# Window scores of a transformer block as 64x64 matmuls, four side by side, with one copy of kT and one signal per tile

## The reference, cut to what matters

```python
h = shift_token(x)
q, k, v = jnp.split(h @ wqkv, 3, axis=-1)          # 8 heads of 64
q, k = rotary_xpos(l2norm(q) * qs, l2norm(k) * ksc)
# windows of 64 tokens; keys are those of the window and of the one before
sim = jnp.einsum('bhwid,bhwjd->bhwij', bq, bk)
mask = (i < j) | (i > j + WINDOW) | (j == -1)
attn = jax.nn.softmax(jnp.where(mask, -jnp.finfo(sim.dtype).max, sim), axis=-1)
out = jnp.einsum('bhwij,bhwjd->bhwid', attn, bv)
x = x + o @ wo
```

## Time and profile before

| | |
|---|---|
| median of 3 runs | 2111.05 us (2105.78 to 2113.18) |
| profiled execution, span | 2108.0 us |
| instructions in it | 46234 |
| TensorE matmul, weight load | 1782.1 us (85%), 1504.1 us (71%) |
| VectorE, ScalarE, GpSimd | 1462.3, 1256.6, 1091.2 us |
| granted TensorE clock | 9 tenths or more in nearly all slices, 7 to 8 between the stacks |

### The profile page before, as it was taken

The page is one execution under the profiler, slowest core; times in us unless marked ns, Lnnn a source line. Parts: engine busy times, 40 slices in busy tenths (PEclk is TensorE's granted clock), DMA queues, the critical chain, the costliest instruction groups (busy, mean ns, idle before and its releaser), DMA issues.

```text
span 2108.0 us, 46234 instructions
## 1 busy us (share of the span) xinstructions
PE 1782.1 (85%) x14712; PEld 1504.1 (71%) x14712; DVE 1462.3 (69%) x3770; ACT 1256.6 (60%) x3443; POOL 1091.2 (52%) x1090
## 2 busy tenths in 40 slices
PE   1899999888999999747756759999998999999984
PEld 1787878777878788625534548878787788888873
DVE  6786868676868687455666548777776767677763
ACT  1686868675868686512311337676766667676771
POOL 3774747464747475321131247565655556665550
PEclk9999999999999999978978879999998999999997
DMA  7221212122112111031010031111112121212113
GB/s 249 85 68 40 48 38 54 44 73 60 45 38 48 41 45 35 12 123 40 0 40 20 10 78 45 39 48 43 46 50 74 39 65 37 49 34 50 33 35 103
DMA packets 183658, 111.91 MB, mean 53 GB/s; under 512 B 86720, under 2 KB 164128, under 8 KB 182944
## 3 DMA queue, kind: packets, MB, share of 16 engines
q1 hardware_dynamic: 183456, 109.12, 19.6%
HBM read 43.41 MB, written 23.42 MB: 32 GB/s over the span
## 4 chain that ended last, share of the span: by engine, by line
PE 69%; DVE 9%; issue 8%; ACT 7%; DMA 3%; SPq 3%; POOL 2%; DVEq 0%; POOLq 0%; ACTq 0%
PE QK L345 12%; PE OB L689 9%; PE SC L611 6%; PE TT L578 6%; PE SC L615 5%; PE VB L345 4%; PE QK L578 4%; PE OB L644 4%; PE TT L345 3%; PE SC L601 3%; ACT probs L1099 2%; PE OB L746 2%; PE VB L746 2%; PE OB L578 2%; PE VB L578 2%
## 5 line engine op out<-in xcount | busy, mean ns | idle before, releaser
L1099 ACT ACTIVATE probs<-SC,shift,qgain 128x128 f32<-128x128 f32 x1024 | 454.3, 457 | 105.1 <-DVE shift L898 104.9
L1225 POOL TENSOR_TENSOR ve<-mv,epsilon 128x1 f32<-128x1 f32 x128 | 24.3, 190 | 614.0 <-DVE mv L942 614.0
L345 PE MATMUL QK<-w_qkv,hT 128*128 128x512 f32 x768 | 227.4, 435 | 49.4 <-issue 16.5
L890 DVE TENSOR_REDUCE top<-SC 128x4 f32<-128x512 f32 x256 | 174.9, 683 | 99.8 <-PE SC L618 97.8
L1093 ACT ACTIVATE kT<-QK 64x512 f32<-64x512 f32 x256 | 150.9, 590 | 121.5 <-PE QK L578 120.0
L951 DVE TENSOR_TENSOR rope_c<-QK,rope 128x512 f32<-128x512 f32 x256 | 174.7, 682 | 68.8 <-PE QK L345 66.3
L578 PE MATMUL TT<-ident,probs 128*128 128x128 f32 x1280 | 193.3, 279 | 29.8 <-ACT probs L1099 23.1
L1238 POOL TENSOR_TENSOR rnorm<-clip,mhalf 128x8 f32<-128x8 f32 x128 | 211.5, 1653 | 12.7 <-DVE clip L907 12.4
L345 PEld LDWEIGHTS QK<-w_qkv,hT 128*128 128x128 f32 x768 | 146.3, 204 | 95.2 <-issue 42.3
L1247 POOL TENSOR_TENSOR qgain<-clip,mhalf 128x8 f32<-128x8 f32 x128 | 209.4, 1636 | 0.7 <-ACT probs L1099 0.5
L1099 ACT ACTIVATION_READ_ACCUMULATOR probs<-SC,shift,qgain 128x1 f32 x1024 | 208.1, 203 | 0.0
(11 more groups left out here) (141 smaller groups left out, 4361.1 us busy)
## 6 DMA issues: line engine op xcount, KB each, us to landing
v_prev<-v_own SPq DMA_DIRECT2D x256, 128.0 KB, 2.3
x_att<-stream SPq DMA_DIRECT2D x128, 64.0 KB, 2.1
h<-stream SPq DMA_DIRECT2D x256, 32.0 KB, 1.9
stream<-x_new SPq DMA_DIRECT2D x32, 256.0 KB
w_qkv<-qkv_d SPq DMA_DIRECT2D x3, 1536.0 KB, 6.5
h<-x_mid SPq DMA_DIRECT2D x128, 32.0 KB
h<-x_mid SPq DMA_DIRECT2D x128, 31.8 KB
rope<-rope_d SPq DMA_DIRECT2D x24, 128.0 KB, 3.3
```

What stands on the lines that cost most here:

```text
L345: last = mm(dst, fr(left(a)), fr(right(b)), start=(k == 0), stop=(k == 2))
L890: v.tensor_reduce(top[:, t.i % 2, 4 * half:4 * half + 4], SC[:, half * 512:half * 512 + 512].rearrange("q (h k) -> q h k", h=4), AX, ALU.m ...
L1099: last = nc.scalar.activation(probs[:, b, hd, :], SC[:, hd * P:hd * P + P], ACT.Exp, bias=shift[:, b, hd:hd + 1], scale=qgain[:, b, hd:hd ...
```

## The change

The scores of a tile are computed in one place, ahead of the products with v, as 16 matmuls of 64 channels x 64 queries x 128 keys (64 keys for the first window of a sequence). For chunk c, window w and head e of the pair, the weights are partitions 64e to 64e + 63 of qT and the output goes to partitions 64w to 64w + 63 of SC, bank e. The even heads' scores so stand in the first bank and the odd heads' in the second, and every later step that goes by heads is reordered: probs and psums are in the order 0, 2, 4, 6, 1, 3, 5, 7, and qgain, pT and rsums are picked to match. kT has no zeros; its four slots of 64 keys are the windows of two tiles, written by one copy of 128 partitions, and the previous window is reached by a slot step of -1 or 3. s_s goes up once per tile instead of twice.

```diff
-        kT = sb("kT", [P, 2, PAIRS, 2, P])
+        kT = sb("kT", [P, PAIRS, 4, WIN])
...
-            def scored(t, half):
+            def scored(t):
 
                 i, b = t.i, t.i % 2
-                sc = SC[:, :].rearrange("q (c e b k) -> q c e b k", c=PAIRS, e=2, b=2)
-                chunks = (2 * half, 2 * half + 1)
-                for c in chunks:
-                    last = mm(sc[:, c, :, 0, :], qT[:, b, c, :], kT[:, b, c, :, 0:64],
-                              start=False, stop=True, skip_group_check=True)
-                for c in chunks:
-                    if i:
-                        last = mm(sc[0:64, c, :, 1, :], qT[:, b, c, 0:64], kT[:, 1 - b, c, :, 64:128],
-                                  start=False, stop=True, skip_group_check=True)
-                for c in chunks:
-                    last = mm(sc[64:128, c, :, 1, :], qT[:, b, c, 64:128], kT[:, b, c, :, 64:128],
-                              start=False, stop=True, skip_group_check=True)
+                sc = SC[:, :].rearrange("q (e c s k) -> q e c s k", e=2, c=PAIRS, s=2)
+                for c in range(PAIRS):
+                    for w in range(2):
+                        for e in range(2):
+                            d, q = slice(64 * e, 64 * e + 64), slice(64 * w, 64 * w + 64)
+                            if w:
+                                keys = kT[d, c, 2 * b:2 * b + 2, :]
+                            elif not i:
+                                keys = kT[d, c, 2 * b:2 * b + 1, :]
+                            else:
+                                keys = kT[d, c, 2:0:-1, :] if b else kT[d, c, 0:4:3, :]
+                            last = mm(sc[q, e, c, 0:keys.shape[1], :], qT[d, b, c, q], keys,
+                                      start=False, stop=True, skip_group_check=True)
                 last.then_inc(s_s, 1)
...
                         need(pe, s_p, t.count(back=1, unit=2))
+                        pe.wait_ge(s_qT, t.count())
+                        pe.wait_ge(s_kT, t.count())
                         masked(t, 0)
                         masked(t, 1)
-                        pe.wait_ge(s_qT, t.count())
-                        pe.wait_ge(s_kT, t.count())
-                        scored(t, 0)
+                        scored(t)
...
-                                          pT[:, hd, 64 * w:64 * w + 64], v[:, t.i, hd * DH:hd * DH + DH],
+                                          pT[:, hd % 2 * 4 + hd // 2, 64 * w:64 * w + 64], v[:, t.i, hd * DH:hd * DH + DH],
...
-                    if t := tile(TQK):
-                        scored(t, 1)
...
-            v.memset(kT[:], 0.0).then_inc(s_zero, 1)
...
-                dve.wait_ge(s_s, t.count(unit=2) + (half - 1))
+                dve.wait_ge(s_s, t.count())
...
-                                       in1=qgain[:, t.i % 2, hd], op0=ALU.mult, op1=ALU.mult).then_inc(s_sh, 1)
+                                       in1=qgain[:, t.i % 2, :].rearrange("p (c e) -> p e c", e=2)[:, half], op0=ALU.mult, op1=ALU.mult).then_inc(s_sh, 1)
...
-                    v.tensor_tensor(o_n[:].rearrange("q (h d) -> q h d", h=HEADS),
-                                    OB[:, :].rearrange("q (h d) -> q h d", h=HEADS),
-                                    rsums[:, b, :].unsqueeze(2).to_broadcast([P, HEADS, DH]), ALU.mult).then_inc(s_on, 1)
+                    v.tensor_tensor(o_n[:].rearrange("q (c e d) -> q c e d", c=PAIRS, e=2),
+                                    OB[:, :].rearrange("q (c e d) -> q c e d", c=PAIRS, e=2),
+                                    rsums[:, b, :].rearrange("q (e c) -> q c e", e=2).unsqueeze(3).to_broadcast([P, PAIRS, 2, DH]),
+                                    ALU.mult).then_inc(s_on, 1)
...
-                    need(act, s_s, t.count(back=1, unit=2))
-                    for e in range(2):
-                        last = copy(kT[64 * e:64 * e + 64, b, :, e, :],
-                                    QK[64 * e:64 * e + 64, 512:1024].rearrange("d (c t) -> d c t", c=PAIRS))
-                    last.then_inc(s_kT, 1)
+                    need(act, s_s, t.count(back=1))
+                    copy(kT[:, :, 2 * b:2 * b + 2, :].rearrange("d c s k -> d c (s k)"),
+                         QK[:, 512:1024].rearrange("d (c t) -> d c t", c=PAIRS)).then_inc(s_kT, 1)
```

More of the change, by code:

```diff
@@ L1099, in exponentials @@
                     last = nc.scalar.activation(probs[:, b, hd, :], SC[:, hd * P:hd * P + P], ACT.Exp,
-                                                bias=shift[:, b, hd:hd + 1], scale=qgain[:, b, hd:hd + 1],
+                                                bias=shift[:, b, hd:hd + 1], scale=qgain[:, b, hd % 4 * 2 + half:hd % 4 * 2 + half + 1],
                                                 accum_out=psums[:, b, hd:hd + 1])
@@ L1275, in _ @@
             pipeline(pool, step, 1)
-ZEROED = 6
+ZEROED = 5
 N_CONST = 16 * 16
```

## The result

The changed kernel takes 2023.26 us (median of 4 runs, 2021.15 to 2025.16) against 2111.43 us (median of four runs of the kernel before, the three above and one more); the ratio is 0.9586, with a 95% interval of 0.9569 to 0.9602. The profiled execution's span is 2022.0 us, 86.0 less than the 2108.0 of the earlier trace rows.

What follows compares the result with a forecast made beforehand. It took a plain step of 10.39 us, a ring through TensorE and ScalarE's copies, as the bound. Per eight steps 5 x 0.67 + 0.3 + 1.0 + 0.45 = 5.1 us, times 16: 82 us, forecast 2028 us, range 1990 to 2080.

Steps and rivals of the forecast that it cites:

- Four abreast: Score matmuls on TensorE: 64x64 matmuls run four at a time, 0.86 us plus 0.33 for shape changes, 1.19 us.
- Rival A: Score matmuls run only two at a time, 0.86 us more per tile; 2135 us in all, chance 0.07.
- rival B: Score weight loads not hidden: rounds of 0.15 instead of 0.107 us, 0.35 us per tile; 2072 us, chance 0.15.
- Rival C: Score matmuls run one at a time, 3.42 + 0.33 us per tile; slower, 2357 us, chance 0.08.
- The point from which it loses: Time for all scores of a tile above which the changed kernel is slower than before: 1.8 us.
- o_n loses its cover: VectorE's o_n, no longer hidden behind the second half of the scores, ends 0.85 us after the products with v.
- TensorE's ring: TensorE's own work in a plain main-loop step, from one QKV product to the next: 9.67 us.
- VectorE's ring with GpSimd: Plain step: shift waits for GpSimd's q_r, and norm and hT wait behind shift, a loop of 9.65 us.
- Rival D: shift slips in before GpSimd's q_r and shape changes cost 0.1 us: plain step 9.45, whole 1997 us, chance 0.10.
- One copy of kT: ScalarE's kT copying falls from 1.18 to 0.60 us, so the copies no longer hold up the QKV product.
- The burst step: Step with a feed-forward burst: earlier transpose of o_n and no second kT copy, 1.0 us gained together.
- The step with the jump: Step at the loop's end: 0.45 us gained before the jump, while the 3.25 us wait for code stays.

Runs made afterwards that it cites:

- the halves: Changed kernel with the 64x64 scores split again, even heads before the products with v and odd heads behind: 2059.3 us, ratio 0.9761.
- runs of four: Changed kernel with the score matmuls reordered, four in a row in the same quarter of the array: 2230.9 us, ratio 1.0569.
- the two copies: Changed kernel with kT copied again as two pieces of 64 partitions: 2087.35 us, ratio 0.9888.
- runs of two: Changed kernel with the score matmuls reordered, two in a row in the same quarter of the array: 2026.48 us, ratio 0.9594.

## Why the prediction was right, point by point

- **Four abreast, and 1.19 us for all scores.** Right: 1.13 us. Rival A, two at a time, is excluded by the slots of the changed kernel and by the halves; rival B, rounds of 0.15 us, by the 0.109 us from one four to the next. Part 3 of the Trainium skill's page "TensorE: Matmul & The Clock Gate" would have weights load beside running matmuls only with another row group. The trace does not bear that out: the second four weight loads start at 518.15 to 518.17, between the first four matmul records (518.10 to 518.12) and the second (518.26 to 518.28), in quarters that share rows. Rival C, that 64-row matmuls exclude each other, is wrong as a rule, but a loss like it lies one loop order away: runs of four take 2.49 us, and that kernel is 120 us slower than the one before the change. The point from which it loses was put at 1.8 us for all scores; the two orders with 1.13 and 2.6 us lie on either side.
- **o_n loses its cover.** Right: expected to end 0.85 us after the products, found at 521.82 - 520.96 = 0.86, and TensorE waits 0.47.
- **TensorE's ring 9.67 us.** It is 9.54. The stretch from the start of o_n's transposes to the QKV product takes 2.62 and not 2.70 us, the one from the end of the products to those transposes 0.91 and not 0.95; none of the sum's terms is off by more than 0.1.
- **VectorE's ring with GpSimd 9.65 us.** It is 9.66. Rival D, in which this ring isn't there, is excluded: shift lasts 0.46 and 0.58 us above and ends with q_r. I took 9.72 for a plain step as if the two rings always disturbed each other; in fact they alternate. The mean gain of a plain step, first tiles among them, was 0.73 us and not 0.61: 70 us over 96 steps where the sum had 58.
- **One copy of kT.** Its place was right, its size too small. I had the second copy at 0.59 us on ScalarE's row, and it is 0.75. In the sum this didn't show, since TensorE binds once it is gone; the two copies show it.
- **The burst step, 1.0 us.** Right: 1.1.
- **The step with the jump, 0.45 us gained.** This is the term that failed: nothing was gained there, and the mean of the 12 steps rose by 0.51. Single ones scatter by 0.5 to 0.9 us, so the size is rough, but the sign of a gain is missing. "3.25 us for code, which stays" didn't hold either. The idle time at the jump that nothing in the profile explains is now 40.0 us over 11 times, before it was 32.9 over 11. In the kernel with the scores in halves, where the same number of matmuls is issued but o_n doesn't keep TensorE waiting ahead of the jump, it is 32.3 over 10:

```profile
PE QK L578 <- issue: 32.3, 10, 3.7
```

  All seven kernels in which o_n holds TensorE up ahead of the jump have a mean of 3.53 to 3.65 us there, the two without that wait 2.99 and 3.23. That fits an instruction stream that reaches the jump only when the wait for o_n is over, where it used to run ahead of the array during the second half of the scores. It is an argument from nine kernels, with code of two sizes; no run took that wait away at the jump alone, and it accounts for 0.65 of the 0.96 us between the forecast and the 12 steps.

The kernel took 2023.26 us where 2028 was forecast. The sum came out 4 us short of the gain in spans (86 against 82), and that it came so near is partly luck, for its errors have both signs. The plain steps gave 70 us for 58, the burst steps 16 for 16. The 16 long steps that the sum took for jumps and gave 7 us lost 1: the 12 with the jump lost 6, the 4 with the wait for weights won 5. What lies outside these steps, which the sum put at nothing, won 1. (Added up, the sum's terms give 2029 us and not 2028: 2108.0 - 82 + 3.) The single signal per tile and the removed memset were not varied alone, and the prediction's nothing either way for the memset stands untested.

## What to carry to other kernels

Matmuls with 64 rows and 64 columns run four at a time if neighbours in the order of issue use different quarters of the array; runs of two in the same quarter did as well within 0.07 us, and runs of four were 1.46 us a tile slower. Look for pairs that are already there: the products with v had them eight matmuls apart, and swapping two loops gave 38 us without any new instruction. When a block is taken away, list what it covered (here o_n, and perhaps a part of the time at the jump), and draw the ring of each engine: after the change TensorE's and that of VectorE with GpSimd were 9.54 and 9.66 us, and ScalarE's showed as 9.29 once the products were shortened. A cut on one is worth no more than the distance to the next.

## What the runs showed that was not expected

- Matmuls in different column halves start out of program order. In the timeline of the kernel before, v_own's first record starts at 549.92 and three records of v_prev that are ahead of it in the program at 549.98, 550.03 and 550.09.
- A copy of 64 partitions costs ScalarE as much as one of 128 (590 against 603 ns a record), and behind another operation a 128x512 copy costs 0.48 us and not 0.60.
- GpSimd's q_r, k_r and k_a hold shift and clip until they end: of the 256 shifts of the changed kernel, 167 last over 0.24 us where a free one takes 0.16, and every one of these ends 0.02 to 0.03 us after a k_r, q_r or k_a. top (0.69 us) and norm (1.21 us) ran beside such operations unhindered, and rnorm and qgain (1.65 us, 8 columns) held nothing up. shift reads two SBUF operands, clip one. The Trainium skill, "SBUF — State Buffer", "SBUF: two separate sides", describes an exclusive lock, for VectorE operations with two SBUF inputs among others, that the one who comes first keeps for its whole instruction. Where GpSimd comes first, the ends of shift and q_r, 0.02 us apart in every pair above, agree with it.
- Where such a small operation falls decides about more than its own length: with the scores 1.46 us longer the first shift ran into q_r, and the step grew by 1.8 us.
